# Causal masking of transposed scores: a minimum on VectorE in place of three products on TensorE, and maxima in groups of eight and four

## The reference

```python
att = jnp.einsum('bhqd,bhkd->bhqk', q, k) * scale          # 12 heads, 324 tokens, head size 16
causal = jnp.tril(jnp.ones((T, T), dtype=bool))
att = jnp.where(causal[None, None], att, -jnp.inf)
sink_col = jnp.broadcast_to(sinks.reshape(1, H, 1, 1), (B, H, T, 1))
att = jnp.concatenate([sink_col, att], axis=-1)
att = jax.nn.softmax(att, axis=-1)[..., 1:]
y = jnp.einsum('bhqk,bhkd->bhqd', att, v)
```

## Time and profile before

| | |
|---|---|
| time of three runs | 2918.97 us median (2916.89 to 2924.98) |
| the profiled execution | 2921.78 us, span 2920.0 us |
| busy in the span | PE 2694.3, PEld 1976.1, DVE 1737.9, ACT 1549.9, POOL 950.7 us |
| granted TensorE clock | 0.968 over the span |
| DMA | 355.46 MB, mean 122 GB/s |

### The profile page before, as it was taken

The page is one execution under the profiler, slowest core; times in us unless marked ns, Lnnn a source line. Parts: engine busy times, 40 slices in busy tenths (PEclk is TensorE's granted clock), DMA queues, the critical chain, the costliest instruction groups (busy, mean ns, idle before and its releaser), DMA issues. The chain is left out here.

```text
span 2920.0 us, 72392 instructions
## 1 busy us (share of the span) xinstructions
PE 2694.3 (92%) x25078; PEld 1976.1 (68%) x25078; DVE 1737.9 (60%) x7898; ACT 1549.9 (53%) x3185; POOL 950.7 (33%) x1814
## 2 busy tenths in 40 slices
PE   6799999999999999999999999999999998699955
PEld 5577777777777777777777777777777775355522
DVE  7466666666666666666666666666666665211133
ACT  2466666666666666666666666666666654111100
POOL 3333333333333333333333333333333332000000
PEclk8899999999999999999999999999999997699988
DMA  4333333333333333333333333333333321699988
GB/s 108 94 96 93 95 99 99 99 98 98 98 96 98 98 97 98 97 96 97 98 98 97 96 98 94 96 94 96 95 94 95 99 81 40 191 318 319 290 240 286
DMA packets 380043, 355.46 MB, mean 122 GB/s; under 512 B 37820, under 2 KB 345021, under 8 KB 379678
## 3 DMA queue, kind: packets, MB, share of 16 engines
q1 hardware_dynamic: 342310, 292.68, 36.1%
q10 hardware_dynamic: 37368, 58.15, 6.4%
HBM read 194.45 MB, written 40.30 MB: 80 GB/s over the span
## 5 line engine op out<-in xcount | busy, mean ns | idle before, releaser
L996 DVE CUSTOM_DVE_ANT_0 ps<-ps,late 128x325 f32<-128x325 f32 (+2 forms) x2304 | 748.5, 395 | 7.9 <-PE ps L474 4.0
L719 ACT ACTIVATE prob<-ps 128x590 f32<-128x590 f32 x768 | 500.8, 660 | 182.4 <-PE ps L497 168.0
L431 PE MATMUL ps<-window_w,xp 108*98 108x193 f32 x2304 | 497.4, 334 | 0.6 <-DVE window_w L953 0.6
L474 PE MATMUL ps<-kst,qst 99*128 99x325 bf16 (+2 forms) x2304 | 330.8, 253 | 38.3 <-DVE negmax L996 31.4
L431 PEld LDWEIGHTS ps<-window_w,xp 108*98 108x98 f32 x2304 | 335.8, 165 | 3.7 <-issue 1.5
L474 PEld LDWEIGHTS ps<-kst,qst 99*128 99x128 bf16 (+1 forms) x2304 | 199.7, 106 | 184.0 <-DVE negmax L996 136.7
L996 DVE DVE_READ_ACCUMULATOR2_ANT negmax<- 128x1 f32 (+1 forms) x2304 | 317.3, 138 | 0.0
L513 PE MATMUL ps<-prob,vaug 128*32 128x324 f32 (+2 forms) x4608 | 285.6, 340 | 0.0
L672 PE MATMUL ps<-xt,wqk 97*128 97x324 f32 (+1 forms) x768 | 251.9, 451 | 1.7 <-ACT xt L719 1.7
L491 PE MATMUL ps<-qst,kst 102*128 102x295 bf16 x768 | 228.8, 298 | 25.4 <-ACT prob L719 22.4
L1188 POOL TENSOR_TENSOR rot<-by 128x324 f32<-128x324 f32 x64 | 56.4, 881 | 599.4 <-DVE by L1095 599.4
(11 more groups left out here) (215 smaller groups left out, 5599.1 us busy)
## 6 DMA issues: line engine op xcount, KB each, us to landing
xw<-in_x_dram SPq DMA_DIRECT2D x384, 189.0 KB
qst<-part SPq DMA_DIRECT2D x768, 60.8 KB
w<-in_L_ffn_fc_weight_dram ACTq DMA_DIRECT2D x32, 1152.0 KB, 10.5
kst<-part SPq DMA_DIRECT2D x384, 81.0 KB
w<-in_L_ffn_fc_weight_dram SPq DMA_DIRECT2D x32, 768.0 KB, 8.7
h_held<-h_new SPq DMA_DIRECT2D x64, 288.0 KB, 3.7
kst<-part SPq DMA_DIRECT2D x768, 20.2 KB
w<-in_L_ffn_fc_weight_dram SPq DMA_DIRECT2D x64, 192.0 KB, 10.7
```

Source lines behind the costliest of these rows:

```text
L431: mm = pe.matmul(ps[0:TILE, BK7, half * (D + 1):(half + 1) * (D + 1)], xp[:, q, TILE * half:TILE * (half + 1)], window_w[:, q, :], start=( ...
L474: mm = pe.matmul(ps[0:nq, bk, col:col + keys], qst[i][0:MAX_ROW, h, q0:q0 + nq], kst[i][0:MAX_ROW, h, 0:keys], start=True, stop=True)
L719: return nc.scalar.activation(out_, in_, f, **kw)
L996: last = dve.tensor_tensor_reduce(out=ps[0:nq, bk, col:col + keys], in0=ps[0:nq, bk, col:col + keys], in1=late[0:nq, gone:gone + keys], sc ...
```

## The change

`scores_t` drops the three causal products and leaves four. In their place VectorE, after the exponentials of each pair of heads, takes the minimum of the exponential and `keep`, a table that holds 3e38 where the key is allowed and 0 where it is not (`mask(b, n)`, n from 0 to 5): 2 x 127 and 2 x 197 elements on each partition. So that the masked columns lie together, the product of `k2` now stands before that of `k1` in PSUM. `values` waits for the masks (`masked`) and no longer for the exponentials. The six calls of `mask` are placed between the steps of VectorE's list. The maxima go in groups of eight and four heads: group 0 is turned behind head 10 of the scores, the turning of `logit` comes behind head 11, and group 1's DMA is awaited at head 8 of `scores_t`. `keep` is made once in the setup from a transpose of the triangle.

```diff
+MAX_GROUPS = [(0, 8), (8, 12)]
+PROB_AT = [0, 393, 324]
+FIRST, REST = 127, 197
...
                     def scores_t(b, i, h):
...
-                        if h in (0, NH // 2):
-                            max_in[h // (NH // 2)].wait(pe, b)
+                        if h in (0, MAX_GROUPS[1][0]):
+                            max_in[min(h, 1)].wait(pe, b)
...
-                        c1, c2 = n0, n0 + T - KTILES[1][2]
-                        pe.matmul(ps[:, bank, 0:EXPC], k0, q[:, 0:EXPC], start=True, stop=False)
-                        pe.matmul(ps[:, bank, 0:127], causal[:], ident_b[:, 1:128], start=False, stop=True)
+                        c1 = n0 + T - KTILES[2][2]
+                        pe.matmul(ps[:, bank, 0:EXPC], k0, q[:, 0:EXPC], start=True, stop=True)
                         pe.matmul(ps[:, bank + 1, 0:n0], k0, q[:, EXPC:T], start=True, stop=True)
-                        pe.matmul(ps[:, bank + 1, c1:c2], k1, q[:, KTILES[1][2]:T], start=True, stop=False)
-                        pe.matmul(ps[:, bank + 1, c1:c1 + 128], causal[:], ident_b[:], start=False, stop=True)
-                        pe.matmul(ps[:, bank + 1, c2:EXPC], k2, q[:, KTILES[2][2]:T], start=True, stop=False)
-                        pe.matmul(ps[:, bank + 1, c2:EXPC], causal[:], ident_b[:, 0:EXPC - c2], start=False,
-                                  stop=True).then_inc(st_mm.sem, 1)
+                        pe.matmul(ps[:, bank + 1, n0:c1], k2, q[:, KTILES[2][2]:T], start=True, stop=True)
+                        pe.matmul(ps[:, bank + 1, c1:EXPC], k1, q[:, KTILES[1][2]:T], start=True, stop=True).then_inc(st_mm.sem, 1)
...
                         if k == 0:
-                            exp_ready.wait(pe, b, 4 * g + 4)
+                            masked.wait(pe, b, 2 * g + 2)
...
-                            if att and h == 8:
+                            if att and h == 10:
                                 v_ready.wait(pe, b + 1, apart=True)
                                 mpart_ready.wait(pe, b, 1)
                                 maxima(b, 0)
-                            if moe and h == 10:
+                            if moe and h == 11:
                                 mt_ready[0].wait(pe, b, apart=True)
...
+                        for at, c0, n in ((0, 1, FIRST), (FIRST, 0, REST - 128), (FIRST + REST - 128, 0, 128)):
+                            dve.tensor_scalar(keep[:, at:at + n], ps[:, BK6, c0:c0 + n], -1.0, LARGEST, ALU.is_ge, ALU.mult)
...
+                    def mask(b, n):
+
+                        exp_ready.wait(dve, b, 2 * n + 2)
+                        heads = prob[:, 2 * n % 8:2 * n % 8 + 2]
+                        for at, c0, nc_ in ((0, 0, FIRST), (FIRST, T, REST)):
+                            some = heads[:, :, c0:c0 + nc_]
+                            last = dve.tensor_tensor(some, some, keep[:, at:at + nc_].unsqueeze(1).broadcast_to((128, 2, nc_)), ALU.min)
+                        last.then_inc(masked.sem, 1)
...
                     def maxima_parts(b, g):
...
+                        lo, hi = MAX_GROUPS[g]
+                        some, left = negmax[:, :, lo:hi], mrest[:, :, 0:hi - lo]
+                        max_ready.wait(pool, b, hi)
```

More of the change, by code:

```diff
@@ L63 @@
 EXPC = 295
+PROB_AT = [0, 393, 324]
+FIRST, REST = 127, 197
 MASKED = -1e30
+LARGEST = 3e38
 NS = 64
@@ L104, in early_fusion_kernel @@
             ident_b = sb("ident_b", [128, 128], BF16, layers)
-            causal = sb("causal", [128, 128], BF16, layers)
+            keep = sb("keep", [128, FIRST + REST], F32, layers)
             late = sb("late", [128, KEYS], F32, layers)
@@ L145, in early_fusion_kernel @@
                 yraw = tmp("yraw", [128, 3, T])
-                negmax, mrest = tmp("negmax", [128, 3, NH]), tmp("mrest", [128, 3, NH // 2])
-                mpart = [tmp(f"mpart{g}", [128, 3, PARTS, NH // 2], BF16) for g in range(2)]
-                mt = [tmp(f"mt{g}", [PARTS * NH // 2, T], BF16) for g in range(2)]
+                negmax, mrest = tmp("negmax", [128, 3, NH]), tmp("mrest", [128, 3, 8])
+                mpart = [tmp(f"mpart{g}", [128, 3, PARTS, hi - lo], BF16) for g, (lo, hi) in enumerate(MAX_GROUPS)]
+                mt = [tmp(f"mt{g}", [PARTS * (hi - lo), T], BF16) for g, (lo, hi) in enumerate(MAX_GROUPS)]
                 rden = tmp("rden", [128, 3, NH])
@@ L158, in early_fusion_kernel @@
                 neg_half, eps = (tmp(n, [128, 3]) for n in ("neg_half", "eps"))
[L159 removed]
+                zero = tmp("zero", [128, 3, 8])
                 logit, lexp = tmp("logit", [128, 3, NS]), tmp("lexp", [128, 3, NS])
@@ L247, in early_fusion_kernel @@
                 max_ready = Signal("max_ready", NH)
+                masked = Signal("masked", NH // 2)
                 yn_ready = Signal("yn_ready", 3)
@@ L509, in values @@
                         _, nk, q0 = KTILES[k]
-                        col = sum(T - KTILES[n][2] for n in range(k))
+                        col = PROB_AT[k]
                         for s in range(4):
@@ L540, in maxima @@
                         for q, (q0, nq) in enumerate(QTILES):
-                            mm = pe.transpose(ps[0:PARTS * NH // 2, (BK6, BK5)[g], :].bitcast(BF16)[:, q0:q0 + nq],
+                            mm = pe.transpose(ps[0:mt[g].shape[0], (BK6, BK5)[g], :].bitcast(BF16)[:, q0:q0 + nq],
                                               mpart[g][0:nq, q].rearrange("p a h -> p (a h)"), ident_b[0:nq, 0:nq])
@@ L565, in prepare @@
                                               ident[0:NS, 0:NS])
+                        pe.wait_ge(const_in, 16 * 15)
+                        mm = pe.transpose(ps[:, BK6, 0:128], causal_f, ident[:])
                         mm.then_inc(slot_mm, 1)
@@ L733, in store_maxima @@
                         st_mm.wait(act, b - 2)
-                        act.dma_start(qst[i][MAX_ROW:STACK, NH // 2 * g:NH // 2 * (g + 1), :], mt[g][:]
+                        act.dma_start(qst[i][MAX_ROW:STACK, MAX_GROUPS[g][0]:MAX_GROUPS[g][1], :], mt[g][:]
                             ).then_inc(max_in[g].sem, 16)
@@ L976, in prepare @@
                         dve.tensor_copy(ident_b[:], ident[:])
-                        dve.tensor_copy(causal[:], causal_f)
                         dve.memset(late[:, 0:KEYS - 128], 0.0)
@@ L1033, in step @@
                             last.then_inc(c_ready.sem, 1)
+                        if att:
+                            mask(b, 0)
                         if moe:
@@ L1038, in step @@
                             dve.tensor_scalar(dexp[:], dexp[:], drec[:, 0:1], None, ALU.mult).then_inc(dn_ready.sem, 1)
+                        if att:
+                            mask(b, 1)
                         if front:
@@ L1047, in step @@
                                 ).then_inc(stat_ready.sem, 1)
+                        if att:
+                            mask(b, 2)
                         if front:
@@ L1058, in step @@
                             norm_stats(h_new[i], bn, mv1).then_inc(ln1_ready.sem, 1)
+                        if att:
+                            mask(b, 3)
                         if moe:
@@ L1065, in step @@
                             last.then_inc(dp_ready.sem, 1)
+                        if att:
+                            mask(b, 4)
                         if front:
@@ L1072, in step @@
                             last.then_inc(xhat_ready.sem, 1)
+                        if att:
+                            mask(b, 5)
                         if moe:
```

14 lines of the change are left out of this document (6 added, 8 removed).

## The result

The changed kernel takes 3194.30 us (median of 4 runs, 3187.10 to 3199.51), the kernel before 2921.97 beside it (4 runs, 2916.89 to 2925.01). The ratio is 1.0932, with a 95% interval of 1.0903 to 1.0961: 9.3% slower. The direction was forecast, the size wasn't: 272 us are lost where 80 were expected, and the range ended at 3080. The profiled execution took 3194.95 us, its span 3193.2.

The account below looks back on a forecast made before the run. TensorE was taken to bound the layer part; mask waits in VectorE's chain, less the saved products, end the second stretch 1.25 us later, times 64 = 80 us, so 2919 + 80 = 2999 us. Eight-in-ten range: 2925 to 3080 us.

Parts of the forecast that it names:

- the likeliest case: The forecast itself: TensorE waits about 1.2 and 1.5 us an image at clock 1.00, 2999 us; chance 0.56.
- a fall there halves the f32 work of the next stretch: 3.4 us of it give 1.7 more: Rival: TensorE's clock falls around `values(1,0)`; 3050 us if in half of the images, 3108 in all; chance 0.22.
- this rival's worst case: TensorE's clock falling around `values(1,0)` in all images: 109 us more, time 3108.
- From `stat` to `h_new` is 2.14, GpSimd's answer; the mask of heads 4 and 5 hides in it: VectorE's chain ahead of `values(1,0)`: 2.14 us waiting for GpSimd's `rstd`, with that mask adding nothing.
- about 0.15 us a head: TensorE's saving from three dropped causal products in `scores_t`: 1.8 us an image, 115 us over 64 images.
- 1.77 without the wait: TensorE's time for transposed-score heads 0 and 1 with window products before the change, forecast to become 1.47 us.
- the lateness of the maxima eats what the first two heads save, and no more: Start of `scores_t`: head 0 starts 0.8 us late for the maxima's DMA, head 2 stays at about 1607.8.
- 1.17 ns an element: VectorE's `tensor_tensor` rate, at most, from the `lexp` rows; gave 0.43 and 0.57 us for a mask pair's two instructions.
- step 5: TensorE reaches `values(1,0)` at 1615.5 and waits 1.5 us, to 1617.1, for the mask of heads 6 and 7.
- step 6: End of the second stretch: heads 10 and 11 save 0.3 us, and the stretch ends 1.25 us later.
- A pair at 1.00 with landings at 2.5 us: Slow end of the forecast's own range: slower mask pairs on VectorE and later DMA landings of the maxima, 3035 us.
- the masks hide, the kernel gets faster: Rival: VectorE's mask pair takes far less than 0.83 us; loss gone at 0.41, 2887 us at 0.25; chance 0.15.

Follow-up runs that it names:

- e1_fill: The changed kernel with 22 and 34 unused TensorE products ahead of the waits of `values(0,0)` and `values(1,0)`: 3023.87 us, 1.0354 of the kernel before.
- e6_mask2thin: The changed kernel with only the mask of heads 4 and 5 cut to one column: 3142.97 us, 1.0761 of the kernel before.
- e10_before_swap: The kernel before the change with ScalarE's exponentials of heads 0 and 1 ahead of `dexp`: 2886.70 us, 0.9882 of the kernel before.
- e9_before_groups: The kernel before the change with only the maxima in groups of eight and four: 2941.15 us, 1.0070 of the kernel before.
- e5_thin: The changed kernel with every mask cut to one column per part, places and waits kept: 2967.20 us, 1.0168 of the kernel before.
- e11: The kernel of e8 with mask 4 moved behind `xhat`: 2955.74 us, 1.0117 of the kernel before.
- e8: The changed kernel with VectorE's list reordered, maxima in groups of six and six, ScalarE's exponentials of heads 0 and 1 before `dexp`: 2919.69 us, ratio 1.0010.
- e12: The kernel of e8 with causal products for heads 8 to 11 and masks only for heads 0 to 7: 2855.55 us, 0.9778 of the kernel before.
- e2_both: The changed kernel with the three causal products put back on TensorE and the masks kept: 3059.98 us, 1.0483 of the kernel before.

## Why the prediction was wrong

**The step that failed** is the one that kept the granted clock out of the likeliest case: "a fall there halves the f32 work of the next stretch: 3.4 us of it give 1.7 more", at a chance of 0.22, against it that "the products around the wait are denser than the scores of the earlier trace rows". The fall came in all 53 images of the layer part from 155 to 2350 us. In the image shown the stretch before it was busy for 1.50 of 3.47 us; in the earlier trace rows a fall had followed 1.98 of 3.41. That row was there, and I argued it away by the density of the products. A fall lasted 6.5 us on the average (344.7 / 53) and not 3.4. The price of 3.4 us, 1.7, was nearly right (1.5 by the images' lengths); how often and how long was not, so that even this rival's worst case, 3108, was 86 us short. Of the 192 us between forecast and result some 170 are the clock and 27 the waits ((1.67 - 1.25) x 64); with the clock kept up, e1_fill came to 3024, inside the range. The Trainium skill ("TensorE: Matmul & The Clock Gate", What's actually happening) has the clock follow how busy TensorE has been recently; e1_fill, with the same waits filled, agrees (1.00, 170 us back). The same page (HAM oscillation — how this bites in real kernels) describes a kernel whose clock swings between its two levels because TensorE waits between bursts. Its waits are some 3 to 5 us long; this trace shows the same swing with single waits of 1.3 and 2.0 us, and the measurement decides.

**Right: the waits and their places.**

| step of the prediction | predicted | measured |
|---|---|---|
| masks' pair, start to next | 0.83 us | 0.82 (1483.30 to 1484.12) |
| wait for the DMA before head 0 | about 0.7 to 0.8 | 0.74, mean 0.68 |
| `mt` to the end of the second mask | 3.09 | 3.04 |
| wait of `values(0,0)` | 1.2 | 1.27 |
| `stat` to `h_new` | 2.14 | 2.70 |
| `h_new` to the release of `values(1,0)` | 2.95 | 2.99 |
| wait of `values(1,0)` | 1.5 | 1.97 |
| an image, clock aside | +1.25 | +1.67 |

**Mis-sized terms.** (a) "From `stat` to `h_new` is 2.14, GpSimd's answer; the mask of heads 4 and 5 hides in it": it fits in the time, but lengthens the answer by 0.56 us; e6_mask2thin shows that this is the mask. (b) Three products "about 0.15 us a head": a head with its two window products now takes 0.61 us (1480.23 to 1480.84) and took 0.81 before (1531.27 to 1532.08), so 0.20. TensorE therefore came to its first wait sooner, which lengthened that wait and saved nothing; from `values(0,0)` to the second wait it took 3.59 us, as in the sum (3.53). The "1.77 without the wait" for heads 0 and 1 was too much as well: it is 1.62 by starts, as e10_before_swap shows. (c) "the lateness of the maxima eats what the first two heads save, and no more": about right, and e9_before_groups prices the groups alone at 19 us.

**Slips in the sum, all small.** 1.17 ns an element gives 0.44 and 0.60 us for the two parts of a mask, not 0.43 and 0.57 (measured 0.41 and 0.56). The terms of step 5 give a wait of 1.56 and those of step 6 a loss of 1.29 us, not 1.5 and 1.25, which is 3 us of time. A pair at 1.00 with landings at 2.5 us gives 3051 by the same sum, not 3035.

**The rival "the masks hide, the kernel gets faster"** put its threshold at a pair of 0.41 us. e5_thin refutes that as a forecast of the time: at 0.14 us it is 1.7% slower than before, since the second wait hangs on what stands ahead of the mask, `h_new`'s statistics and, with VectorE earlier, an input's DMA; and this wait lets the clock fall. My sum had moved the whole chain forward with the pair and had no row for the DMA. The busy shares (6.7 us idle for 5.0 us of masks) would have promised a gain; the order forbade it.

**What stays open.** Why a fall lasts 3.4, 6.8 or 10.2 us, with TensorE busy throughout, no run here explains. Nor is e11's excess over e8 split between its waits and its clock, nor e12's gain over e10 between masks and order.

## What to carry to other kernels

Work moved to an engine with idle time must fit its queue at the place where the consumer needs it: follow the chain in order, and put the work ahead of what waits on another engine. Where a change makes TensorE wait for 1 to 2 us in every iteration, price the granted clock as a case of its own: here it cost more than the waits, and 56 useless products an image were worth 170 us. If neither engine can take all of a job, split it at the point where its consumers stop waiting: with the same swap on ScalarE, masks for eight heads and products for four (2856 us) beat products for all (2887) and masks for all (2920).

## What the runs showed of the hardware

GpSimd's steps with two f32 inputs in SBUF stretch while VectorE runs a `tensor_tensor` on two SBUF inputs: 196 to 787 ns for a step of 98x2, 866 to 1423 for a power of 128x3. In the timeline L1202 starts at 1485.74 and ends at 1486.53, just after the two mask instructions that began at 1485.59 (end 1486.47): it looks blocked, not slowed in proportion, though no run tests which. The Trainium skill ("SBUF — State Buffer", Who interferes with whom) states that a VectorE instruction with two SBUF inputs contends with a GpSimd instruction that reads SBUF, and this trace agrees, with the 0.59 us above.

TensorE's clock fell once an image with waits of 1.3 and 2.0 us, nearly never (6.8 us in all) in e2_both with shorter ones (112.4 us in 124), and not at all in e9_before_groups, whose new wait is 0.7 us on the average. The length of the longest wait doesn't settle it alone: in e8_best none in the repeating part is over 1.2 us, and 61.4 us ran at half clock.
